# A hybrid transformer block on one core: its second half as one program of numbered steps, and GpSimd normalising the tokens of the two mixtures of experts

## The reference

```python
x = x + attn_a(_layernorm(x))    # test-time training: 2 gradient steps with Newton-Schulz on three
                                 # 128x512 weights, then for the queries q (16 heads of 8, unit length):
                                 #   h_q = swish(q @ gate) * (q @ val);  o = h_q @ proj @ proj_w + proj_b
x = x + ffn(_layernorm(x))       # 8 experts of 128x128, the best 2 per token
x = x + attn_b(_layernorm(x))    # 16 heads of 64, mask by frames of 32 tokens within each 512
x = x + ffn(_layernorm(x))       # the same experts again

def _L0_ffn_ref(x, We, be, Wg, bg):
    gates = jax.nn.softmax(x_flat @ Wg + bg, axis=-1)
    topk_gates, topk_idx = jax.lax.top_k(gates, K)
    topk_gates = topk_gates / jnp.sum(topk_gates, axis=1, keepdims=True)
    expert_out = jnp.einsum('nd,edo->neo', x_flat, We) + be
    selected = jnp.take_along_axis(expert_out, topk_idx[:, :, None], axis=1)
    out = jnp.sum(selected * topk_gates[:, :, None], axis=1)
```

## Time and profile before

| what | us |
|---|---|
| median of three runs (lowest, highest) | 866.03 (865.5, 868.25) |
| the profiled execution's own time | 866.14 |
| its span, first to last instruction | 863.7 |
| PE busy (matmul) / weight loads | 774.2 (90%) / 616.6 (71%) |
| DVE / ACT / POOL busy | 545.4 (63%) / 394.9 (46%) / 270.7 (31%) |
| mean granted TensorE clock | 0.940 |

### The profile page before, as it was taken

How to read it: one execution, slowest core, us unless ns; L and a number is a source line. 1 busy time by engine, 2 the same in 40 slices (tenths; PEclk the granted TensorE clock), 3 DMA queues, 4 the chain that set the end, 5 groups by cost and what they waited for, 6 DMA issues and landing times. The chain is left out here.

```text
span 863.7 us, 15529 instructions
## 1 busy us (share of the span) xinstructions
PE 774.2 (90%) x5512; PEld 616.6 (71%) x5512; DVE 545.4 (63%) x1649; ACT 394.9 (46%) x1118; POOL 270.7 (31%) x476
## 2 busy tenths in 40 slices
PE   3669999897999988987858999999999999999786
PEld 1239999775999976677645677777777777777765
DVE  3945656444555535664796776776677666665468
ACT  4733333243333234312255766565556555564224
POOL 4830000002445002100372444343334333333027
PEclk9969999997999999895898999999999999999678
DMA  3040000000000000000000000000000000000001
GB/s 104 1 134 1 1 2 1 1 1 1 1 1 2 1 1 1 0 1 1 0 2 0 2 2 2 2 2 1 2 2 1 2 2 2 2 1 2 1 0 50
DMA packets 9466, 7.17 MB, mean 8 GB/s; under 512 B 1584, under 2 KB 9008, under 8 KB 9264
## 3 DMA queue, kind: packets, MB, share of 16 engines
q1 hardware_dynamic: 9392, 6.19, 2.3%
HBM read 5.14 MB, written 1.05 MB: 7 GB/s over the span
## 5 line engine op out<-in xcount | busy, mean ns | idle before, releaser
L1295 POOL TENSOR_SCALAR t_p_<-t_p_,t_rinv_ 128x128 f32<-128x128 f32 (+3 forms) x256 | 132.1, 532 | 202.3 <-DVE t_rinv_ L1491 202.3
L1325 ACT ACTIVATE t_p_<-t_p_,t_nmin_ 128x128 f32<-128x128 f32 (+3 forms) x256 | 140.0, 551 | 9.1 <-DVE t_nmin_ L1484 9.1
L1484 DVE CUSTOM_DVE_ANT_0 t_p_<-t_S_,t_mask_ 128x128 f32<-128x128 f32 (+3 forms) x256 | 112.8, 487 | 21.7 <-PE t_S_ L1382 17.3
L1330 ACT ACTIVATE t_pT_<-t_T_ 128x384 f32<-128x384 f32 (+1 forms) x96 | 50.5, 526 | 118.3 <-PE t_T_ L1394 118.3
L1394 PEld LDWEIGHTS t_T_<-ident,t_p_ 128*128 128x128 f32 x640 | 68.2, 141 | 44.9 <-issue 26.0
L1382 PE MATMUL t_S_<-t_k_,t_q_ 64*128 64x256 f32 (+3 forms) x512 | 95.0, 468 | 0.1
L1394 PE MATMUL t_T_<-ident,t_p_ 128*128 128x128 f32 x640 | 90.8, 281 | 0.3 <-ACT t_pT_ L1330 0.3
L1409 PEld LDWEIGHTS t_O_<-t_pT_,t_v_ 128*64 128x64 f32 x1280 | 69.2, 137 | 11.0 <-ACT t_pT_ L1330 10.5
L1409 PE MATMUL t_O_<-t_pT_,t_v_ 128*64 128x128 f32 x1280 | 76.9, 275 | 0.0
L522 DVE SCALAR_TENSOR_TENSOR g_sw<-g_th,g_G 128x512 f32<-128x512 f32 x32 | 22.0, 688 | 71.3 <-ACT g_slope L436 66.2
L1382 PEld LDWEIGHTS t_S_<-t_k_,t_q_ 64*128 64x128 f32 x512 | 41.5, 185 | 26.9 <-DVE t_nmin_ L1484 12.3
(11 more groups left out here) (259 smaller groups left out, 1794.5 us busy)
## 6 DMA issues: line engine op xcount, KB each, us to landing
wqkv<-in_L_attn_b_w_qkv_dram SPq DMA_DIRECT2D x1, 1536.0 KB
x<-in_L_attn_a_x_dram SPq DMA_DIRECT2D x4, 256.0 KB, 4.2
out_dram<-x SPq DMA_DIRECT2D x4, 256.0 KB, 2.3
we<-in_L_ffn_We_dram SPq DMA_DIRECT2D x1, 512.0 KB
wout<-in_L_attn_b_w_out_dram SPq DMA_DIRECT2D x1, 512.0 KB
proj<-n_L_attn_a_ttt_proj_dram SPq DMA_DIRECT2D x1, 256.0 KB, 5.3
gv<-n_L_attn_a_ttt_gate_dram SPq DMA_DIRECT2D x1, 256.0 KB, 4.9
gv<-in_L_attn_a_ttt_val_dram SPq DMA_DIRECT2D x1, 256.0 KB, 5.4
```

The source lines that it names most:

```text
L1295: last = pool.tensor_scalar(pr[:, G.par, h, cols], pr[:, G.par, h, cols], rinv[:, G.par, n:n + 1], 1.0, ALU.mult, ALU.mult)
L1325: act.activation(pr[:, G.par, h, cols], pr[:, G.par, h, cols], ACT.Exp, bias=nmin[:, G.par, n:n + 1], scale=-1.0, accum_out=rsum[:, G.par, ...
L1330: act.activation(pT[:, G.par, 0, G.blocks], psT[:, 0, 0:G.width], ACT.Copy).then_inc(t["eA"], 1)
L1484: dve.tensor_tensor_reduce(pr[:, G.par, h, cols], psS[:, (2 * G.n + h) % 3, at_:at_ + keys], mask[:, SEQ - keys:SEQ], 1.0, -NEG, ALU.add, ...
```

## The change

`query_phase`, `moe_phase` and `attention_phase` are gone. One `second_half_phase` replaces them, without a barrier inside: every engine walks through the same steps, from -52 to 117, and lists say in which step each piece of work is issued. Attention's 96 groups keep steps 0 to 95. The queries' chunks go in steps -50 to -18, two steps each. The experts are done in four jobs: batches 0 and 1 before the attention (steps -16 to -9), batches 2 and 3 beside its first eight steps, and, in the second mixture, batches 0 to 2 (steps 96 to 107) and batch 3 (steps 108 to 115). Routing is done for a job's two or three batches at once, with DVE's small instructions spread over four steps.

Other edits: PSUM is three banks that all uses share in turn (projections, outputs, pair products, transposed tokens, logits, biases, experts), with three for scores and two for transposes that the last experts also use; swish is one activation on ACT and one DVE multiplication fewer; the low part of the queries moves from DVE to POOL; 1/sqrt is a power on POOL instead of ACT's square root and DVE's reciprocal; POOL normalises the tokens of the experts; four experts are weighed on ACT (five instructions of DVE become four), and POOL adds them as one 256-column and one 128-column addition; y, z, a and b have two buffers, the first sum one, and `close` comes one step late; outputs are made in two halves of four products; biases are stored for one batch rather than four.

```diff
+                pool.memset(self.mhalf[:, :], -0.5).then_inc(self.s_bias, 1)
...
+    class Job:
+        BATCHES = ((0, 2), (2, 4), (0, 3), (3, 4))
+        TOPS = (-24, -8, 86, 106)
+        FILLS = (tuple(range(-16, -8)), tuple(range(0, 8)),
+                 (96, 97, 98, 99, 99, 101, 102, 102, 103, 105, 105, 106), (108, 108, 108, 111))
+        SUMS = (tuple(range(-16, -8)), tuple(range(0, 8)),
+                (96, 97, 98, 99, 100, 102, 103, 104, 104, 105, 106, 107), (112, 113, 114, 115))
...
+            self.weights = self.top + (5 if j < 2 else 4)
+            self.bias = self.top + (7 if j < 2 else 5)
...
+        def lower(self, n):
+            return Kernel.Job.FILLS[self.j][n] + (3 if (self.j, n) == (3, 2) else 0)
...
+        def weighed(self, n):
+            return self.summed(n) - (1 if self.j == 3 else 0)
...
-            psS, psT, psO, psP = ps("S", [P, 3, 512]), ps("T", [P, 2, 512]), ps("O", [P, 512]), ps("P", [P, 2, 512])
+            psS, psT, psP = ps("S", [P, 3, 512]), ps("T", [P, 2, 512]), ps("P", [P, 3, 512])
+            psG, psU, psO = psS[:, 0:2, :], psT, psS[:, 2, :]
...
+            QUERY = -50
+            ANSWER = 9
+            STEPS = range(QUERY - 2, Job.SUMS[-1][-1] + 3)
+            IN_BATCH = NP * self.NG
+            Q_STEPS = [-6] + [3 * p for p in range(self.PAIRS - 1)]
+            K_STEPS = [-5] + [3 * p + 1 for p in range(self.PAIRS - 1)]
+            V_STEPS = [-4, -3, -2, -1] + [3 * n + 2 for n in range(2 * BATCH * TPB - TPB)]
+            X_STEPS = [-8] + [IN_BATCH * b + 12 for b in range(BATCH - 1)]
+            OUT_STEPS = [IN_BATCH * b + step for b in range(BATCH)
+                         for step in (17, 18, 19, 20) + ((29, 30, 31, 32) if b < BATCH - 1 else (29, 29, 29, 29))]
+            M_STEPS = [QUERY + 2 * NC * b + 12 for b in range(BATCH)] + [34, 58, 82, 102]
+            N_STEPS = [s + 1 for s in M_STEPS]
+            T_STEPS = [s + (3 if s < 0 else 2) for s in M_STEPS]
+            L_STEPS = [s + (5 if s < 0 else 3) for s in M_STEPS]
...
+                return spare[kind, n][0] if (kind, n) in spare else psP[:, place[kind, n] % 3, :]
...
+                if at_ >= 3:
+                    kind_, n_ = uses[at_ - 3]
+                    sem, times = emptied[kind_]
+                    e.wait_ge(sem, (n_ + 1) * times)
...
+                def power(kind, n, b):
+                    pool.wait_ge(t["var"], norm_of[kind, n] + 1)
+                    rows = slice(b * TPB, b * TPB + TPB)
+                    pool.tensor_tensor(self.rstd[:, rows], self.lnw[:, 3, rows], self.mhalf[:, rows], ALU.pow).then_inc(t["root"], 1)
+
+                def norm(c):
...
+                    for n in range(TPB):
+                        r = c % BATCH * TPB + n
+                        last = pool.tensor_scalar(mn[:, c % 2, n, :], x[:, r, :], self.mean[:, r:r + 1], self.rstd[:, r:r + 1],
+                                                  ALU.subtract, ALU.mult)
...
+                def add_experts(J, n):
+                    i = J.index(n)
+                    pool.wait_ge(m["y"], i + 1)
+                    if i:
+                        pool.wait_ge(m["z"], i)
+                    pool.tensor_tensor(half[:, :, :], y[:, i % 2, 0:2, :], y[:, i % 2, 2:4, :], ALU.add).then_inc(m["z0"], 1)
+                    pool.wait_ge(m["z0"], i + 1)
+                    if i > 1:
+                        pool.wait_ge(m["s"], 4 * (i - 2) + 2)
+                    pool.tensor_tensor(z[:, i % 2, :], half[:, 0, :], half[:, 1, :], ALU.add).then_inc(m["z"], 1)
+
+                def close(J, n):
+                    i = J.index(n)
+                    pool.wait_ge(m["s"], 4 * i + 4)
+                    pool.tensor_tensor(x[:, J.row(n), :], a[:, i % 2, :], b_[:, i % 2, :], ALU.add).then_inc(m["x"], 1)
+
+                def low_q(b):
+                    pool.wait_ge(q["qh"], b + 1)
+                    pool.tensor_tensor(ql[:, b % 2, :], self.qkT[:, 0, b * SEQ:b * SEQ + SEQ], qh[:, b % 2, :].bitcast(F32),
+                                      ALU.subtract).then_inc(q["ql"], 1)
...
+                for s in STEPS:
...
+                    for J, n in tiles(s - 1, Job.summed):
+                        close(J, n)
+                    for J, n in tiles(s, Job.weighed):
+                        add_experts(J, n)
...
-                act.preload_act_table(ACT.Exp)
+                act.preload_act_table(ACT.Silu)
...
+                def gates(J):
+                    act.wait_ge(m["sh"], J.j + 1)
+                    if J.j:
+                        act.wait_ge(m["c"], J.j)
+                    act.activation(gate[:, J.rows, :], logit[:, J.rows, :], ACT.Exp).then_inc(m["e"], 1)
...
+                def weigh(pair):
+                    b, p = divmod(pair, NP)
+                    wait_bank(pe, "pv", pair)
+                    pe.wait_ge(t["ve"], b * 8 + (p // TPB) * TPB + TPB)
...
+                def accumulate(J, n):
...
+                    for e in range(4):
+                        acc = (a, b_)[e % 2][:, i % 2, :]
+                        if e == 1:
+                            dve.wait_ge(m["z"], i + 1)
+                        if e > 1:
+                            dve.wait_ge(m["s"], 4 * i + e - 1)
+                        so_far = (x[:, J.row(n), :], z[:, i % 2, :])[e] if e < 2 else acc
+                        dve.scalar_tensor_tensor(acc, bank("el", i)[:, tile_of(e)], weight(e), so_far,
+                                                 ALU.mult, ALU.add).then_inc(m["s"], 1)
...
-            k.query_phase()
-        k.moe_phase(0)
-        k.attention_phase()
-        k.moe_phase(1)
+        k.second_half_phase()
```

More of the change, by code:

```diff
@@ L1265, in attention_phase, with planned, values, outputs @@
[L1265 removed]
+            def planned(steps, s):
+                return [n for n, step in enumerate(steps) if step == s]
+            def values(s):
+                return [(i // 8, i // TPB % 2, i % TPB) for i in planned(V_STEPS, s)]
+            def outputs(s):
+                return [(i // 8, i // TPB % 2, i % TPB) for i in planned(OUT_STEPS, s)]
+            def query(s, step):
+                b, n = divmod(s - QUERY - step, 2 * NC)
+                return b if n == 0 and 0 <= b < BATCH else None
@@ new lines, in chunk, with jobs, tiles @@
+            def chunk(s, lag=0):
+                n, odd = divmod(s - QUERY - lag, 2)
+                return n if not odd and 0 <= n < BATCH * NC else None
+            def jobs(s, steps):
+                return [Job(j) for j in planned(steps, s)]
+            def tiles(s, when):
+                return [(Job(j), n) for j in range(NJ) for n in range(Job(j).nt) if when(Job(j), n) == s]
+            spare, last_use = {}, {}
+            free = [psS[:, 0, :], psS[:, 1, :], psS[:, 2, :], psT[:, 0, :], psT[:, 1, :]]
@@ new lines, in second_half_phase @@
+            order = [0, 1, 2]
+            for s in STEPS:
+                if s == Job.FILLS[2][0] + LT:
+                    order = [3, 4] + order
+                for kind, when in (("eh", Job.upper), ("el", Job.lower)):
+                    for J, n in tiles(s, when):
+                        if J.j == 2 or J.j == 3 and s < J.bias:
+                            at_ = order.pop(0)
+                            spare[kind, J.index(n)] = (free[at_], last_use.get(at_), at_ > 2)
+                            last_use[at_] = (kind, J.index(n))
+                            order.append(at_)
@@ new lines, in _ @@
+                    for b in planned(X_STEPS, s):
+                        turn_x(b)
+                    for c in planned(T_STEPS, s):
+                        turn_tokens(c)
+                    for c in planned(L_STEPS, s):
+                        logits(c)
+                    for J in jobs(s, W_STEPS):
+                        turn_weights(J)
+                    for c in planned(B_STEPS, s):
+                        biases(c)
+                    for J, n in tiles(s, Job.upper):
+                        experts(J, n, "eh", 512, m["H"])
@@ L1446, in _ @@
+                    for J, n in tiles(s, Job.lower):
+                        experts(J, n, "el", 0, m["E"])
+                    if query(s, ANSWER) is not None:
+                        answer(query(s, ANSWER))
                     if O and O.g == 2:
-                        for g in range(self.NG):
-                            weigh(Group(O.n - 2 + g))
-                for m in range(TPB):
-                    output(BATCH - 1, m)
+                        weigh(O.pair)
             @block.vector
```

900 lines of the change are left out of this document (451 added, 449 removed).

## The result

The changed kernel takes **905.6 us** (four runs, 901.0 to 909.0) against 866.7 us for the kernel before on the same chip: a ratio of 1.044, 95% interval 1.039 to 1.050. It is slower by 39 us; 833 us, faster, had been predicted. The profiled execution took 904.58 us, span 902.8.

The account below looks back on a forecast made before the run. PE's work at full clock was the floor, a POOL-DVE ring the limit where experts are alone. From span 863.7 us, 32.6 gained before attention, 24.2 lost in it, 24.3 gained at the end: span 831.0, time 833, range 813 to 856.

Parts of the forecast that it names:

- The moments, norms and routing of these batches lie beside the queries ... and cost nothing: Queries, batches 0 to 2: this work hides beside PE's query products (a step about 1.1 us of PE), adding 0.
- without that cover each batch would show about 6 us: Queries: cost of each batch's moments, norms and routing if PE's query work did not hide them, about 6 us.
- POOL's norm at 0.372 us: POOL's norm of one token tile takes 0.372 us; four for the last batch, 1.5 us, stand in the end's ring.
- DVE now ends each of these steps with a wait for POOL's sum ... 2 us in eight steps (bounds 0 and 8): Attention steps with expert tiles: the next tile's lower bank waits 0.3 us a step, 2 us in all, bounds 0 and 8.
- The ring: Experts alone: POOL's close and two sums, then DVE's last three sums, in strict order, take 2.7 us a tile.
- serial chain: Rival, 8%: PE gets a bank only when DVE has finished the tile before; 20 tiles at 5.2 us, 883.
- PE's added work in attention, 22.2 us: Attention: second job's tiles 11.1, bias 0.7, tokens and logits 5.7, outputs 1.8, third job's weights and biases 2.9; paid in full.
- the predicted 35.4 and 50.5: Lengths in us: first experts (394.6) to first scores (430), and the end, shrinking from 74.8 to 50.5.
- lie beside: End: pair product, outputs, statistics and logits of batch 3 hide beside the third job's tiles.
- The clock rival (843): Rival, 20%: PE's clock falls where the ring rules and after idle seams, adding 10 us, 843.
- near 0.97 was expected: Sign that the prediction is right: PE's granted clock near 0.97.
- the predicted 831.0: Span of the changed kernel, 831.0 us, 32.7 less than 863.7.

Follow-up runs that it names:

- Experiment 6: Changed kernel with tokens transposed six steps later and the queries' high and low parts made three steps earlier; 885.0 us, ratio 1.023.
- Experiment 8: The mended kernel with the tokens' norm back on POOL, at the step the change had it; 860.0 us, ratio 0.994.
- mended kernel: Changed kernel with upper halves, weighings, POOL's sums a step ahead; close after sums; tokens transposed later, normalised by DVE; query parts earlier; attention's tokens later; 849.0 us.
- experiment 4: Changed kernel with each tile's upper half, its weighing and POOL's sums one step earlier in the first three jobs; 883.7 us, ratio 1.020.
- Experiment 9: The mended kernel with POOL's close of the tile before put back ahead of the sums, as in the change; 845.4 us, ratio 0.976.
- Experiment 10: The mended kernel with upper half, weighing and POOL's sums back in the same step as DVE's sums; 867.9 us, ratio 1.003.
- experiment 1: Changed kernel with POOL adding tile i before it closes tile i-1, instead of after; 905.4 us, ratio 1.043.
- experiment 5: Changed kernel with the attention's token work for batches 0 and 1 five steps later; 905.5 us, ratio 1.046.

## Why the prediction was wrong

- **"The moments, norms and routing of these batches lie beside the queries ... and cost nothing": the step that failed first.** I compared sums of work, not distances. The working itself had the price, "without that cover each batch would show about 6 us", and did not hold it against the cover: six steps of 0.7 us, 4.2 in all, against a chain of 8.3. At the prediction's own price for the norms (1.5 us, and nothing for the power) the chain would still be 5.6, longer than the cover. Experiment 6 gives back 19 of the 29 us of this stage. At the end the same word failed again: the last pair's product and the outputs "lie beside", and they and batch 3's chain open a distance of 10.12 us between two closes.
- **POOL's norm at 0.372 us.** The earlier trace rows has POOL's multiplication by one column; the norm takes two (mean and inverse deviation), and each took 0.79. I had not priced the power at all: 1.03. Per batch the chain on POOL is 4.2 us, not 1.5. Experiment 8 measures 11 us for POOL's norm in the mended kernel, all of it in attention and the end. Whether the second column or the subtraction makes it longer than the earlier trace rows no run separates.
- **"DVE now ends each of these steps with a wait for POOL's sum ... 2 us in eight steps (bounds 0 and 8)".** Measured 14 us (25.7 less PE's 12), undone by experiment 4. The ring's period was taken from a stretch with experts alone; in attention POOL's normalising with its own wait stands in the same list. The rival "serial chain" had this mechanism, a bank freed by DVE's sums of the tile before, and I gave it 8% and put it at the wrong tiles.
- **PE's added work in attention, 22.2 us.** Experiment 9 has PE 349.4 us busy in attention at full clock, against 323.4 before: 26.0. The tiles were right. The outputs were not: 224 records instead of 192, so 32 more of 0.113 us and not 16; and a batch's tokens make steps 33 to 48 in experiment 9 3.4 us longer, 2.3 of PE's work with its changes of kind (1.9 predicted) and 1.1 of waits.
- **The ring of 2.7 us a tile was right as a period** (2.65 where it is alone), and not as what a tile costs: the means are 3.96 and 3.69, since power, norms, PE's waits and the last outputs stand in or between the rounds. Experiment 9 takes 33.3 us from first experts to first scores and 51.1 from the last scores to the end, near the predicted 35.4 and 50.5, but that doesn't confirm the sum: there the upper half is a step ahead, and in both jobs closes come down to 1.6 us apart or less. Experiment 10, without that lead, takes 58.5 in the end even with VectorE's norms. That the two stages come near their predictions after the mends is luck.
- **The clock rival (843)** had the level right, and in part the place: the first job's clock is 0.71 and its stage 6 us over the forecast. The larger loss was behind the waits in the queries (0.75), where it had not looked. The mean clock is 0.940, and near 0.97 was expected.

Experiment 9's span of 844.3 us is 13.3 over the predicted 831.0: 8.6 in the queries, 6.6 in attention (4 of PE's work, the rest in the main waits for row minima) and 1.0 ahead of the queries, less 2.1 in the first job and 0.8 in the end. In the queries PE still waits 3.5 for the routing and 3.3 for the tokens' low parts, in experiment 9 as in experiment 6, whose lines these are:

```profile
PE t_P_ L1376 <- DVE t_mwt_ L1591: 3.5, 1, 3.5
PE t_P_ L115 <- DVE t_ml_ L1535: 3.3, 3, 1.4
PE t_S_ L115 <- POOL t_xl_ L1127: 1.6, 1, 1.6
```

Whether a better place for the first routing removes them wasn't tried.

## What to carry to other kernels

When work is put "beside" other work in engines with strict order, don't compare busy times: take the two instructions between which it must fit, write down the chain's length and the cover's length in the same microseconds, and do it for every list that the chain blocks, not only PE's. A helper engine's operation that waits (here the power) holds everything behind it in its list. Before a tile's producer, helper and consumer are put in one step, look at who frees the bank: one step of lead cost nothing and was worth 19 to 22 us.

## What the runs showed of the hardware that was not expected

- POOL took 0.79 us for a 128x128 instruction with two scalar columns, against 0.372 with one in the earlier trace rows, and 1.03 for a power over 128x4; both hardly varied (787 to 798 ns in 32 instructions, 1017 to 1046 in 12). The two 128x128 instructions also differ in their operations (subtract and multiply against two multiplications), so the number of columns isn't shown to be the cause.
- A stage in which PE often waits can vary by its clock alone: the same instructions from first query to first expert took 72.1, 77.1 and 77.4 us in three executions (experiment 1, the changed kernel, experiment 5). PE waited 17.6, 16.7 and 17.0 us in them and was busy 56.4, 61.5 and 61.8, at a clock of 0.82, 0.75 and 0.75. The attention, at full clock, repeated within some tenths but for the 1.6 us named above.
- Small DVE instructions stretch beside POOL. At step 34 of the changed kernel, POOL first, then DVE:

```profile
605.55 1.39 POOL L1088 TENSOR_SCALAR t_p_<-t_p_,t_rinv_ 128x512 f32<-128x512 f32 x2 [1.56 <-DVE t_rinv_ L1489]
...
605.75 0.54 DVE L1443 TENSOR_TENSOR lnw<-stats 128x4 f32<-128x4 f32 x1
606.32 0.63 DVE L1444 SCALAR_TENSOR_TENSOR lnw<-lnw 128x4 f32<-128x4 f32 x1
606.99 0.17 DVE L1445 TENSOR_SCALAR lnw<-lnw 128x4 f32<-128x4 f32 x1
```

L1443 and L1444 took 0.17 and 0.16 us in the queries (at 360.28 and 360.48), and here 0.54 and 0.63: they have two inputs in SBUF, and the second ends at 606.95, when POOL's pair ends at 606.94; L1445, behind POOL's pair, takes 0.17 again. In all six places where these two ran beside POOL they took 0.31 to 0.64 us, and 0.16 to 0.17 in the six without it; the reciprocal over 128x4 (L1489), with one input, took 0.16 to 0.17 beside POOL and without it. The Trainium skill, "SBUF — State Buffer", section "SBUF: two separate sides", says that such a DVE instruction and one of GpSimd share a pair of ports under an exclusive lock, held for a whole instruction. This trace agrees, with the six places just given. In the prediction I had weighed contention for POOL's sums, and it was DVE's chain that paid.
